# Attention of a two-layer LSTM decoder with the context as the stream, through column tiles of TensorE, and the gates of the fed-back vector placed behind all score products

## What is computed

```python
def step(carry, x_t):
    h0, c0, h1, c1, a = carry
    xin = jnp.concatenate([x_t, a], axis=-1)
    h0, c0 = _lstm_cell(xin, h0, c0, Wi0, Wh0, bi0, bh0)
    h1, c1 = _lstm_cell(h0, h1, c1, Wi1, Wh1, bi1, bh1)
    q = h1 @ Wq.T
    attn = jax.nn.softmax(jnp.einsum('bh,bsh->bs', q, context), axis=-1)
    mixed = jnp.einsum('bs,bsh->bh', attn, context)
    a2 = jnp.tanh(jnp.concatenate([mixed, h1], axis=-1) @ Wo.T + bo)
    return ((h0, c0, h1, c1, a2), a2)
```

## Time and profile before

| | us |
|---|---|
| median of 3 runs | 1902.4 (1902.16 to 1904.66) |
| the profiled execution | 1905.45 |
| its span in the trace | 1903.7 |
| TensorE busy | 1474.6 (77%) |
| VectorE busy | 1184.7 (62%) |
| ScalarE busy | 761.3 (40%) |
| GpSimd busy | 209.3 (11%) |
| recurrence, about 600 to 1520 us | 920 |

### The profile page before, as it was taken

The page is one execution under the profiler, slowest core; times in us unless marked ns, Lnnn a source line. Parts: engine busy times, 40 slices in busy tenths (PEclk is TensorE's granted clock), DMA queues, the critical chain, the costliest instruction groups (busy, mean ns, idle before and its releaser), DMA issues. The chain is left out here.

```text
span 1903.7 us, 82660 instructions
## 1 busy us (share of the span) xinstructions
PE 1474.6 (77%) x34335; PEld 1281.8 (67%) x34336; DVE 1184.7 (62%) x4397; ACT 761.3 (40%) x1849; POOL 209.3 (11%) x427
## 2 busy tenths in 40 slices
PE   1547777777734999999999999999999874039997
PEld 0446666666613888888888888888888763026665
DVE  5878888888785665666566566566656575014444
ACT  2446566656564343343344334334333311013332
POOL 0000000000001000000000000000000001743333
PEclk9778888899856999999999999999999855569999
DMA  6000000000034000000000000000000070222222
GB/s 210 1 2 0 0 0 0 0 0 0 1 89 201 2 0 0 0 0 0 0 0 0 0 0 0 0 0 0 0 0 0 4 229 20 103 80 72 71 71 51
DMA packets 42813, 57.39 MB, mean 30 GB/s; under 512 B 5754, under 2 KB 32892, under 8 KB 40856
## 3 DMA queue, kind: packets, MB, share of 16 engines
q1 hardware_dynamic: 36672, 42.90, 7.5%
q0 software_dynamic: 5376, 12.66, 1.9%
q10 hardware_dynamic: 728, 1.34, 0.2%
HBM read 30.52 MB, written 26.88 MB: 30 GB/s over the span
## 5 line engine op out<-in xcount | busy, mean ns | idle before, releaser
L1518 DVE TENSOR_TENSOR hb<-psH,b_sb 128x512 f32<-128x512 f32 x72 | 49.8, 692 | 168.9 <-issue 89.2
L900 PE MATMUL sc_a<-h_a,KH 128*128 128x32 f16 (+1 forms) x4096 | 122.7, 176 | 2.5 <-DVE h_a L1058 2.5
L940 PEld LDWEIGHTS mx_a<-pmv_a,VH 128*128 128x128 f16 x4096 | 106.8, 96 | 25.0 <-DVE pmv_a L1087 24.7
L940 PE MATMUL mx_a<-pmv_a,VH 128*128 128x32 f16 (+1 forms) x4096 | 112.8, 176 | 13.8 <-DVE pmv_a L1087 13.6
L940 PEld LDWEIGHTS mx_b<-pmv_b,VH 128*128 128x128 f16 x4096 | 106.7, 96 | 24.9 <-DVE pmv_b L1087 24.9
L940 PE MATMUL mx_b<-pmv_b,VH 128*128 128x32 f16 (+1 forms) x4096 | 112.6, 176 | 13.8 <-DVE pmv_b L1087 13.8
L900 PE MATMUL sc_b<-h_b,KH 128*128 128x32 f16 (+1 forms) x4096 | 121.7, 176 | 0.0
L860 PE MATMUL z_a<-h_a,WL 128*128 128x64 f16 x2304 | 112.7, 194 | 9.6 <-DVE h_a L1050 1.9
L860 PE MATMUL z_b<-h_b,WL 128*128 128x64 f16 x2304 | 112.4, 193 | 9.5 <-issue 1.1
L900 PEld LDWEIGHTS sc_a<-h_a,KH 128*128 128x128 f16 x4096 | 112.0, 96 | 2.7 <-DVE h_a L1058 2.6
L462 PE MATMUL psK<-ident,xn 128*128 128x128 f32 x64 | 21.6, 338 | 117.7 <-DVE VB L667 91.1
(11 more groups left out here) (282 smaller groups left out, 3775.1 us busy)
## 6 DMA issues: line engine op xcount, KB each, us to landing
sorted_x<-zt SPq DMA_DIRECT2D x9, 1032.0 KB, 11.9
xr<-sorted_x SPq DMA_DIRECT2D x72, 65.0 KB
xg<-sorted_x SPq DMA_DIRECT2D x72, 64.0 KB
XT<-in_ctxT SPq DMA_DIRECT2D x1, 4096.0 KB, 13.1
x_scratch<-X SPq DMA_DIRECT2D x1, 4096.0 KB, 15.9
TOK<-x_scratch SPq DMA_DIRECT2D x4, 1024.0 KB, 9.9
w_sb<-in_w SPq DMA_DIRECT2D x1, 2048.0 KB, 12.8
b_sb<-in_b SPq DMA_DIRECT2D x1, 2048.0 KB, 20.1
```

The source lines that it names most:

```text
L900: mm = nc.tensor.matmul(A.S[:, WIDE * n:WIDE * n + streamed(n)], KH[:, k, pair * P:(pair + 1) * P], A.h[1][:, 2 * n:2 * n + streamed(n) // ...
L940: mm = nc.tensor.matmul(A.M[:, WIDE * n:WIDE * n + streamed(n)], VH[:, k, pair, :], A.pm[:, n, 0:streamed(n)], start=False, stop=False, sk ...
L1518: nc.vector.tensor_tensor(hb[:, u, :], psH[:, u, :], b1_sb[:, bass.ds(col, FF)], ALU.add).then_inc(v_hb, 1)
```

## The change

Scores: `h` of layer 1 is written into a zeroed window `hw`, one column for each sequence, 32 columns apart, so that 32 neighbouring columns, taken at a shift, hold h in the wanted column and zeros elsewhere. Those 32 columns are now the weights, the sequence's 64 context columns are the stream, and the product goes to one of four column tiles (`QUAD * t`); a tile gathers 16 x 2 sequences in 32 rows and columns `0:T` of the bank. The products of the high part come first, 128, then 64 of the low part, behind its wait. Mixing is turned round in the same way: weights are 32 columns of the window `pm`, the stream is the 128 columns of `VH`; row halves and column tiles make eight tiles, 128 products.

The softmax now has rows on all 128 partitions instead of 64, with 64 columns each; `d` is scaled and shifted ahead of the exponential, and a diagonal `dg` times `p` normalises and turns at once. The row sums are copied by VectorE and ScalarE (`mr`) and turned back by two products with `fold`, which add to the `WO2` products in `out`; the output tanh reads that directly.

Order: `WA0` gates come after all score products; `early0x` after the mixing; `cell(0)` comes ahead of the maximum as before, and `hidden_low(1)` behind the copy `mr`. GpSimd copies h of layer 1 (`h1`) for `early1` and `WO2`. The masks `smask`, `pmask`, `II` go, `pick` and `fold` come, the zero tile `zt` is half as wide and stored in twice as many DMAs.

```diff
-WIDE = 512 // GP
-STREAM = 2 * WIDE
-PAD = (STREAM - 4) // 2
-NSPLIT = 24
+QUAD = 32
+NQ = P // QUAD
+HALFQ = QUAD // 2
+EIGHT = QUAD // 4
+H_AT = HALFQ - 1
+P_AT = HALFQ - 2
...
+        hw = [sbr(f"hw_{t}", [P, 2, GB, QUAD], F16) for t in "ab"]
+        pw2 = [sbr(f"pmw_{t}", [P, GP, QUAD], F16) for t in "ab"]
...
+                @block.gpsimd
+                def _(pool):
+                    for g in range(2):
+                        pool.memset(hw[g][:, :, :, :], 0.0).then_inc(g_win, 1)
+                        pool.memset(pw2[g][:, :, :], 0.0).then_inc(g_win, 1)
+                    pool.wait_ge(g_win, 4)
...
-                q.h = [sb(f"h{l}_{t}", [P, GB + PAD, 2], F16) for l in range(2)]
+                q.h0 = sb(f"h0_{t}", [P, GB, 2], F16)
+                q.hw = hw[g]
+                q.h1 = sb(f"h1_{t}", [P, 2, GB], F16)
...
+                q.pm = pw2[g]
+                q.mr = sb(f"mr_{t}", [P, 2, D])
...
+                q.pT = q.S[:, T:T + GP]
+                q.rows = [q.M[:, 0:D], q.S[:, P:P + D]]
+                q.out = q.M[:, 2 * P:2 * P + GB]
...
-                    def streamed(n):
-                        return min(STREAM, 512 - WIDE * n)
+                        gates(q, 1, WH1, [q.h1[:, k, :] for k in range(2)])
+
+                    def scores(q, k, parts):
+
+                        for i in range(HALFQ):
+                            for part in parts:
+                                for t in range(NQ):
+                                    b = 2 * (HALFQ * (t % 2) + i) + t // 2
+                                    at = b * QUAD + H_AT - i
+                                    mm = nc.tensor.matmul(q.S[QUAD * t:QUAD * (t + 1), 0:T],
+                                                          q.hw[:, k, :, :].rearrange("p b w -> p (b w)")[:, at:at + QUAD],
+                                                          KH[:, part, (q.g * GB + b) * T:(q.g * GB + b + 1) * T],
+                                                          start=(k == 0 and i == 0 and part == 0),
+                                                          stop=(k == 1 and i == HALFQ - 1), skip_group_check=True)
+                        return mm
+
+                    def mixing(q):
+
+                        win = q.pm[:, :, :].rearrange("p n w -> p (n w)")
+                        for i in range(EIGHT):
+                            for part in range(2):
+                                for j in range(NQ):
+                                    n = EIGHT * j + i
+                                    at = n * QUAD + P_AT - 2 * i
+                                    for h in range(2):
+                                        mm = nc.tensor.matmul(q.rows[h][QUAD * j:QUAD * (j + 1), :],
+                                                              win[T * h:T * (h + 1), at:at + QUAD],
+                                                              VH[T * h:T * (h + 1), part, q.g * GP + n, :],
+                                                              start=False, stop=False, skip_group_check=True)
+                        return mm
 
                     def half(L, A, lt, at):
                         last = isinstance(at, int) and at == T - 1
-                        def scores(n0, n1):
-                            for n in range(n0, n1):
-                                pair = A.g * GP + n
-                                for k in range(2):
-                                    mm = nc.tensor.matmul(A.S[:, WIDE * n:WIDE * n + streamed(n)],
-                                                          KH[:, k, pair * P:(pair + 1) * P],
-                                                          A.h[1][:, 2 * n:2 * n + streamed(n) // 2, :].rearrange("p b k -> p (b k)"),
-                                                          start=(k == 0), stop=(k == 1))
-                            return mm
+                        if A:
+                            pe.wait_ge(A.s_h[1], 2 * at + 1)
+                            scores(A, 0, (0, 1))
                         if A:
                             pe.wait_ge(A.s_h[1], 2 * at + 2)
-                            scores(0, NSPLIT)
+                            scores(A, 1, (0,)).then_inc(A.s_sc, 1)
                         if L:
 
                             gates_as_ready(L, 0, WA0, [L.a[:, :, k] for k in range(2)], L.s_ah, lt).then_inc(L.s_z[0], 1)
                         if A:
-                            scores(NSPLIT, GP).then_inc(A.s_sc, 1)
                             if not last:
                                 early0h(A)
-                            pe.wait_ge(A.s_sm, at + 1)
-                            for k in range(2):
-                                mm = nc.tensor.matmul(A.S[0:64, 0:64], A.sm[:, :, k], II[:, :],
-                                                      start=(k == 0), stop=(k == 1))
-                            mm.then_inc(A.s_st, 1)
+                            pe.wait_ge(A.s_hc, at + 1)
                             if not last:
                                 early1(A)
                         if L:
 
-                            gates_as_ready(L, 1, WI1, [L.h[0][:, 0:GB, k] for k in range(2)], L.s_h[0],
+                            gates_as_ready(L, 1, WI1, [L.h0[:, :, k] for k in range(2)], L.s_h[0],
                                            lt + 1).then_inc(L.s_z[1], 1)
                         if A:
-                            pe.wait_ge(A.s_pe, at + 1)
-                            nc.tensor.transpose(A.S[:, 128:256], A.pe[:, :], ident[:, :]).then_inc(A.s_pt, 1)
+                            pe.wait_ge(A.s_dg, at + 1)
+                            for h in range(2):
+                                mm = nc.tensor.matmul(A.pT[T * h:T * (h + 1), :], A.p[:, :], A.dg[:, h, :],
+                                                      start=True, stop=True)
+                            mm.then_inc(A.s_pt, 1)
+                            for k, (w, m) in enumerate(((0, 0), (1, 0), (0, 1))):
+                                if k == 2:
+                                    pe.wait_ge(A.s_pm, 2 * at + 2)
+                                nc.tensor.matmul(A.out, WO2[:, w, :], A.h1[:, m, :],
+                                                 start=(k == 0), stop=False, skip_group_check=True)
+                            mixing(A).then_inc(A.s_mx, 1)
                             if not last:
                                 early0x(A, at + 1)
-                        if A:
-                            for k, (w, m) in enumerate(((0, 0), (1, 0), (0, 1))):
-                                nc.tensor.matmul(A.Mv[:, :, :, 0], WO2[:, w, :],
-                                                 A.h[1][:, 0:GB, m].rearrange("p (n b) -> p n b", b=2),
-                                                 start=(k == 0), stop=False, skip_group_check=True)
-                            pe.wait_ge(A.s_pm, 2 * at + 2)
-                            for n in range(GP):
-                                pair = A.g * GP + n
-                                for k in range(2):
-                                    mm = nc.tensor.matmul(A.M[:, WIDE * n:WIDE * n + streamed(n)], VH[:, k, pair, :],
-                                                          A.pm[:, n, 0:streamed(n)],
-                                                          start=False, stop=False, skip_group_check=True)
-                            mm.then_inc(A.s_mx, 1)
+                            pe.wait_ge(A.s_me, at + 1)
+                            pe.wait_ge(A.s_mo, at + 1)
+                            for h in range(2):
+                                mm = nc.tensor.matmul(A.out.rearrange("p (n h) -> p n h", h=2)[:, :, h], A.mr[:, h, :],
+                                                      fold[:, :], start=False, stop=False, skip_group_check=True)
+                            mm.then_inc(A.s_ar, 1)
...
-                            act.wait_ge(A.s_nm, at + 1)
-                            nc.scalar.activation(A.p[:, :], A.S[0:64, 0:64], ACT.Exp, bias=A.nm[:, 0:1],
+                            act.wait_ge(A.s_d, at + 1)
+                            nc.scalar.activation(A.p[:, :], A.d[:, :], ACT.Exp,
                                                  accum_out=A.sum[:, 0:1]).then_inc(A.s_ex, 1)
                         if L:
                             gate_tanh(1)
                             out_gate(1)
                             cell_tanh(1)
                         if A:
+                            act.wait_ge(A.s_mx, at + 1)
+                            nc.scalar.activation(A.mr[:, 1, :], A.rows[1], ACT.Copy).then_inc(A.s_mo, 1)
                             act.wait_ge(A.s_ar, at + 1)
                             wait(act, A.s_ao, at)
-                            nc.scalar.activation(A.a32[:, :], A.ar[:, :], ACT.Tanh, bias=bo_sb[:, 0:1],
+                            nc.scalar.activation(A.a32[:, :], A.out, ACT.Tanh, bias=bo_sb[:, 0:1],
```

(43 more changed lines are left out.)

84 lines of the change are left out of this document (35 added, 49 removed).

## The result

The changed kernel takes **2597.8 us** (median of 4 runs, 2577.0 to 2615.6), the kernel before, on the same chip, 1902.3 (1901.4 to 1904.7): 1.365 times as long, 95% interval 1.354 to 1.376. The forecast was 2020 us, 1950 to 2125. The direction was right, and 578 us are missing.

The account below looks back on a forecast made before the run. The prediction took a closed loop through TensorE's fixed order in the recurrence as the bound: 2.32 + 3.70 + 2.03 = 8.05 us a half against 7.09, 127 times, net +119 us, 2020 us (1950 to 2125).

Parts of the forecast that it names:

- third rival: Supply of TensorE's code in the recurrence: a long run gets one product per 0.0125 us, 2218 us; chance 0.07.
- second rival: TensorE's clock drops in new idle time; at a mean of 0.86, 0.72 us more a half, 2111 us; chance 0.12.
- sum of 8.05 us: One half (one group's two layers, the other's attention) after the change: 2.32 + 3.70 + 2.03 us, against 7.09.
- Leg A: In each half, change of shape, scores and fed-back gates, up to the gate tanh: 2.32 us.
- change of shape: TensorE switching tile shape, on entering and leaving scores and mixing: 0.10 us each (0.06 to 0.15).
- Leg B: From the gate tanh through cell(0), softmax and turned weights to the f16 writes: 3.70 us against 3.25.
- Leg C: Third output product, mixing, x gates, row-sum copies and fold, up to the next scores: 2.03 us against 1.61.
- The moved gates: Twelve gate products of the fed-back vector now follow all scores on TensorE, 0.36 us, making the gate tanh start later.
- The first 1.20 is new waiting: On VectorE the finished scores lie unread behind the other group's cell(0), 1.20 us from gate tanh to maximum.
- Tiles without rounds: Score and mixing products paced at 0.0046 us each instead of by rounds: some 1898 us, or 1878; chance 0.15.
- Tiles not side by side: Score and mixing products in different tiles still cost the present 0.0252 us each: some 2735 us; chance 0.03.
- Hidden work: Strided writes of layer 1's h, 0.2 to 0.3 us slower, hidden: h ready about 0.8 us before TensorE is free.

Follow-up runs that it names:

- a_full_fill: a_mix1_same with twelve extra 256-column products a half in TensorE's waits, body 90 KB: 2088.8 us, 1.097 of the kernel before.
- a_mix1_same: Changed kernel with the 64 mixing products of the context's low part replaced by five 256-column products into unused columns, body 87 KB: 2196.9 us.
- a_wide_fill: Changed kernel, whole computation, high-part score products taking both context parts as one 128-column stream, VectorE adding the parts, twelve extra products in waits, 89 KB: 2094.1 us.
- a_half: Changed kernel without the products of the context's low part (64 of the scores, 64 of the mixing a half), body 69 KB: 2026.2 us.
- a_half_fill: a_half with twelve extra 256-column products a half, into unused columns, where TensorE waits, body 73 KB: 1950.9 us.
- a_wide_mid: a_wide_fill with the twelve gate products of the fed-back vector moved back between the high-part and low-part score products: 2031.5 us, 1.068 of the kernel before.
- b_gates_last: Kernel before with all 64 score products ahead of the twelve gate products of the fed-back vector: 1933.2 us, 1.015 of before.
- a_half_nm: a_half with VectorE taking the maximum and the subtraction ahead of cell(0) of the other group: 2014.8 us.
- a_straight: Changed kernel with TensorE's 128 halves written out in full, no loop or branch: 2590.8 us.

## Why the prediction was wrong

The sum had no term for bringing TensorE's code, and the runs put 401 us there. The 693 us between 1904.6 (the kernel before, beside a_full_fill) and 2597.8 divide by the runs into three:

| step | us |
|---|---|
| the work, kept and at full clock (a_full_fill, 2088.8) | 184 |
| the clock (a_mix1_same, 2196.9) | 108 |
| the code (the changed kernel, 2597.8), with the clock that its stops cost | 401 |

The last row is a difference to a stand-in: the five wide products are not the 64 that they replace, but a_wide_fill, with the whole computation, is 5 us from a_full_fill. The time of a_mix1_same is one run; the pair a_half and a_half_fill, with less work, gives 75 us for the clock.

**The code, 401 us.** This is the step that failed: the sum took it that TensorE's instructions are there when their turn comes. The forecast saw the body grow from 206 to 397 products and argued in its third rival that "the code queue moved 0.36 MB in all, so the body is not fetched anew in each pass now". That is true of 53 KB and says nothing about 102. The rows bound what is kept from below only, and the forecast took them as a licence. The rival then priced slow supply as an even pace, 2218 us, with a chance of 0.07. What the changed kernel shows is no slower even pace: in the recurrence TensorE stands still 112 times for 1.5 to 4.0 us, 287 us together, and the products between run at the pace of their clock. And 4.8 pieces a pass (303 in the recurrence) are 78 KB, most of the body, though it is at most 7 KB larger than one that is kept.

**The clock, 108 us.** The second rival, and it held beside the first. The forecast priced it at 0.72 us a half, for a mean clock of 0.86, and measured are 9.37 - 8.51 = 0.86 at 0.85 (average halves of a_mix1_same and a_full_fill). Its reason, new idle time, was right: filling the waits with twelve products of 0.11 us gave the clock back, and ahead of the second layer's gates the wait is 1.09 us in a_full_fill (1204.85 to 1205.94), forecast 1.1. What failed was the chance of 0.12, and setting it against the forecast instead of adding it to the sum.

**The sum of 8.05 us.** The kernel to hold it against is a_full_fill, 8.42 in the steady part. Its timeline for legs A and B:

```profile
1201.85 1.76 PE L902 MATMUL sc_b<-KH,hw_b 128*32 128x64 f16 x192
...
1204.11 0.47 ACT L985 ACTIVATE gt_a<-z_a,sc 128x256 f32<-128x256 f32 x1 [1.75 <-PE z_a L864]
...
1205.01 0.23 DVE L1076 SCALAR_TENSOR_TENSOR c_a<-u_a 128x64 f32<-128x64 f32 x1
1205.15 0.22 DVE L1100 TENSOR_REDUCE nm_b<-sc_b 128x1 f32<-128x64 f32 x1
...
1205.40 0.34 DVE L1103 TENSOR_SCALAR d_b<-sc_b,nm_b,sc 128x64 f32<-128x64 f32 x1
...
1205.78 0.26 ACT L1003 ACTIVATE p_b<-d_b 128x64 f32<-128x64 f32 x1 [0.26 <-DVE d_b L1103]
...
1206.28 0.15 DVE L1110 RECIPROCAL r_b<-sum_b 128x1 f32<-128x1 f32 x1
...
1206.47 0.25 DVE L1112 TENSOR_SCALAR dg_b<-pick,r_b 128x64 f32<-128x64 f32 x1
...
1206.78 0.31 PE L954 MATMUL sc_b<-dg_b,p_b 128*64 128x32 f32 x4
...
1207.13 0.30 DVE L1115 CAST pmw_b<-sc_b 128x32 f16<-128x32 f32 x1 [0.41 <-PE sc_b L954]
...
1207.82 0.20 PE L961 MATMUL mx_b<-h_b,WO 128*128 128x64 f16 x1
```

- Leg A, from the first score product to the gate tanh: 1204.11 - 1201.85 = 2.26. The forecast's 2.32 begins 0.10 earlier, with the change of shape; without it, it is 2.22. A score product takes 8.3 ns, 33 ns a round of four; forecast 32.
- Leg B, to the product that waits for both writes: 3.71, forecast 3.70. cell(0) held VectorE for 1.04 (1.20), the subtraction to the exponential took 0.38 (0.25), the exponential 0.50 (0.44), the diagonal 0.31 (0.28), the turn 0.35 (0.40), the two writes 0.69 (0.69). The errors cancel, which is luck.
- Leg C is what remains, 8.42 - 2.26 - 3.71 = 2.45, forecast 2.03 and the 0.10 of the change, 2.13. Its rows, from a_wide_fill, whose mixing is the changed kernel's:

```profile
1201.32 0.20 PE L964 MATMUL mx_a<-h_a,WO 128*128 128x64 f16 x1
...
1201.45 0.23 PE L921 MATMUL mx_a<-VH,pmw_a 64*32 64x128 f16 x1
...
1202.02 0.45 DVE L1088 TENSOR_TENSOR hw_b<-os_b,tc_b 128x64 f16<-128x64 f32 x1 [0.32 <-ACT tc_b L998]
...
1202.49 0.22 PE L921 MATMUL sc_a<-VH,pmw_a 64*32 64x128 f16 x1
...
1202.65 0.52 PE L866 MATMUL z_a<-xs_a,WL 128*128 128x64 f16 x12
...
1202.77 0.28 ACT L1013 ACTIVATE mr_a<-sc_a 128x128 f32<-128x128 f32 x1 [0.79 <-PE sc_a L921]
...
1203.19 0.60 PE L972 MATMUL mx_a<-fold,mr_a 128*128 128x32 f32 x4
...
1203.73 1.59 PE L905 MATMUL sc_b<-KH,hw_b 128*32 128x128 f16 x128
```

Mixing takes 1.04 us from first to last product instead of 0.90: 8.2 ns a product, 66 a round of eight, where the forecast halved L509's f32 round and took 56. The change of shape behind it is 0.16 (0.10), the x gates with the wait for the copies 0.54 (0.45), the fold with the change behind it 0.54 (0.44 + 0.10). Together 0.29 of the missing 0.32; the stand-in of a_full_fill is 0.05 longer than this mixing. With 0.05 from legs A and B, the mis-sized terms come to 8.42 - 8.05 = 0.37 us a half, 47 us. The first three halves of a_full_fill take 11 us more than steady ones, against 1.4 before, by the halves' lengths, and the first output tanh comes 4 us later than before where 3 less were forecast (why, no run shows): together some 16, and 119 + 47 + 16 = 182 of the table's 184.

**The moved gates.** The forecast carried their cost in legs A and B and never gave it by itself; a_wide_mid puts it at 0.50 us a half and b_gates_last at 0.22 in the old kernel. "The first 1.20 is new waiting" was right as a description and wrong as a cause: taking the wait away in a_half_nm brought 0.09.

**Tiles without rounds** (the faster side, 0.15) is refuted: a product costs 8.2 to 8.3 ns in long runs, not L449's 4.6. But the forecast's reason against it, that the stream sets the pace, holds only at the start. By the single starts in a_full_fill the first four score products come 3 to 4 ns apart and the first ten rounds mostly 29 ns apart; from about the 40th product on they come singly, 7 to 10 ns apart, nearly all rounds at 32 to 35. Mixing in a_wide_fill does the same: rounds of 56 ns twice among the first four, then 66 to 67. L449's run of 32 products ends before that. So the third rival's doubt about a pace seen over 32 products was right in kind, and that the forecast's 32 ns came so near the measured 33 is partly luck. **Tiles not side by side**: also refuted, and with it the rule in the Trainium skill, "TensorE: Matmul & The Clock Gate", section "Wait — 56ns, not 53.3ns?", that starts are never closer than about 25 ns; for products in different tiles they are three times as close at full clock here (8.2 to 8.3 ns).

**Hidden work.** The strided write of h takes 0.45 us (1202.02 in the last fence) instead of 0.23, as forecast, and is done at 1202.47, over a microsecond ahead of the scores at 1203.73. That is the high part; the low part's write ends at 1203.41 (0.43 us from 1202.98), also ahead of them. It costs nothing.

## What to carry to other kernels

Count the instructions of the longest loop body on TensorE, before and after a change (the other engines were not tried). More and smaller products can take less time in the array (mixing 1.04 us instead of 1.61) and still lose all of it, and a row that shows no refetch at one size is no word on a larger size. Idle time that a change opens on TensorE has a second price, its clock, which belongs in the sum; extra products in the waits gave it back here. A short run of products is no measure of a long one either. And where two roads meet at one instruction, price a wait by both of them before calling it the cause.

## What the runs showed of the hardware

- TensorE's code stays for loop bodies of 53, 69, 73, 86, 87, 89, 90 and 95.5 KB (22 to 30 pieces in the whole run) and does not for 102 and 106 KB (319 and 295). Fresh code comes in pieces of 16.4 KB, 3.3 to 5.6 us apart in a_straight, 4.1 KB per us. A branch back takes 0.21 us in the loops whose code is kept; in the two others it takes 3.7 to 4.6, but in the changed kernel only each second time, else 0.23. Why the changed kernel's passes alternate between the two was not tried.
- Adding 12 products of 256 columns to each half made a kernel 75 us faster (a_half, a_half_fill); its granted clock went from 0.87 to 1.00 in the stretch 650 to 1500 us.
- Products with 32-column weights in different tiles, in long runs at full clock: 8.3 ns each in four tiles with 64-column streams (33 a round) and 8.2 in eight tiles with 128-column streams (66 a round), so there the product sets the pace, whatever its stream. The first ten rounds or so of four go at 29 ns. In four tiles with 128 columns the stream sets it, 56 ns a round, 14 a product (64 products in a_wide_fill).
- At 1.2 GHz the same score products start 13 ns apart in the changed kernel, 53 ns a round of four, evenly over 127 of them.
